# A transformer block in fp32: the first token tiles are split into high and low parts straight from PSUM, and the plain products are issued part by part

## What is computed

```python
def ffn(x, w_gate, w_up, w_down):          # 512 -> 2048 -> 512
    gate = einsum('bsd,hd->bsh', x, w_gate)
    up = einsum('bsd,hd->bsh', x, w_up)
    return einsum('bsh,dh->bsd', silu(gate) * up, w_down)

x = x + 0.5 * ffn(layernorm(x), w_gate, w_up, w_down)
x = x + attn(layernorm(x), W, lam_logit, eta, gamma, beta)   # z = x W', scan, layernorm
x = x + 0.5 * ffn(layernorm(x), w_gate, w_up, w_down)
```

## Time and profile before

| | |
|---|---|
| median of 3 runs | 1061.6 us |
| the profiled execution | 1061.71 us |
| its span in the trace | 1059.9 us |
| TensorE matmul busy | 1048.4 us, 99% |
| VectorE busy | 644.2 us, 61% |
| ScalarE busy | 352.3 us, 33% |
| GpSimd busy | 113.2 us, 11% |
| share of the chain that ended last on TensorE | 96% |

### The profile page before, as it was taken

The page is one execution under the profiler, slowest core; times in us unless marked ns, Lnnn a source line. Parts: engine busy times, 40 slices in busy tenths (PEclk is TensorE's granted clock), DMA queues, the critical chain, the costliest instruction groups (busy, mean ns, idle before and its releaser), DMA issues.

```text
span 1059.9 us, 12841 instructions
## 1 busy us (share of the span) xinstructions
PE 1048.4 (99%) x4756; PEld 867.6 (82%) x4756; DVE 644.2 (61%) x969; ACT 352.3 (33%) x585; POOL 113.2 (11%) x127
## 2 busy tenths in 40 slices
PE   8999999999999999999999999999999999999998
PEld 8788888878888888888888888888888888888886
DVE  5955765567677657878657865687665323233342
ACT  6545544425322222222623222222333332222311
POOL 3322343120020110001002001000000000000000
PEclk9999999999999999999999999999999999999999
DMA  6399877666656556556546555565566566556264
GB/s 196 123 339 339 319 256 262 249 228 199 211 194 211 179 179 199 190 179 212 164 134 227 181 193 179 171 206 179 186 212 217 191 195 200 179 187 210 81 222 164
DMA packets 56845, 215.80 MB, mean 204 GB/s; under 512 B 5840, under 2 KB 15056, under 8 KB 48848
## 3 DMA queue, kind: packets, MB, share of 16 engines
q1 hardware_dynamic: 56640, 214.98, 59.8%
q10 hardware_dynamic: 144, 0.00, 0.0%
HBM read 170.92 MB, written 44.04 MB: 203 GB/s over the span
## 4 chain that ended last, share of the span: by engine, by line
PE 96%; DMA 2%; DVE 1%; DVEq 0%; POOL 0%; issue 0%; SPq 0%
PE ps_a L1275 8%; PE ps_a L1277 8%; PE ps_a L1276 8%; PE ps_b L1277 8%; PE ps_b L1276 8%; PE ps_b L1275 8%; PE ps_d L1275 6%; PE ps_d L1277 6%; PE ps_d L1276 6%; PE ps_c L1275 6%; PE ps_c L1277 6%; PE ps_c L1276 6%; PE aux L1277 3%; PE aux L1275 3%; PE aux L1276 3%; DMA dn<-dn_kept 1%
## 5 line engine op out<-in xcount | busy, mean ns | idle before, releaser
L829 DVE TENSOR_TENSOR tmp<-tmp,ps_c 128x512 f32<-128x512 f32 x59 | 40.5, 687 | 140.4 <-PE ps_c L1277 140.4
L1275 PE MATMUL ps_a<-xt,gu 128*128 128x512 f32 x308 | 121.2, 394 | 2.3 <-DVE gu L873 1.5
L1277 PE MATMUL ps_a<-xt,gu 128*128 128x512 f32 x308 | 120.0, 390 | 0.0
L1276 PE MATMUL ps_a<-xt,gu 128*128 128x512 f32 x308 | 119.9, 389 | 0.0
L1275 PE MATMUL ps_b<-xt,gu 128*128 128x512 f32 x288 | 112.6, 391 | 0.0
L1277 PE MATMUL ps_b<-xt,gu 128*128 128x512 f32 x288 | 112.1, 389 | 0.0
L1276 PE MATMUL ps_b<-xt,gu 128*128 128x512 f32 x288 | 112.1, 389 | 0.0
L1275 PE MATMUL ps_d<-dn,hid 128*128 128x512 f32 x256 | 100.8, 394 | 0.0
L1277 PE MATMUL ps_d<-dn,hid 128*128 128x512 f32 x256 | 99.8, 390 | 0.0
L1276 PE MATMUL ps_d<-dn,hid 128*128 128x512 f32 x256 | 99.7, 389 | 0.0
L1275 PE MATMUL ps_c<-xt,gu 128*128 128x512 f32 x238 | 92.9, 390 | 0.0
(11 more groups left out here) (227 smaller groups left out, 2044.8 us busy)
## 6 DMA issues: line engine op xcount, KB each, us to landing
dn<-dn_kept SPq DMA_DIRECT2D x112, 512.0 KB, 3.3
gu<-gu_kept SPq DMA_DIRECT2D x46, 1024.0 KB, 5.0
gu<-gu_kept SPq DMA_DIRECT2D x46, 768.0 KB, 5.4
gu_kept<-gu SPq DMA_DIRECT2D x16, 1024.0 KB, 4.6
gu_kept<-gu SPq DMA_DIRECT2D x16, 768.0 KB, 4.2
dn_kept<-dn SPq DMA_DIRECT2D x16, 512.0 KB, 5.1
zw<-zw_kept SPq DMA_DIRECT2D x16, 512.0 KB, 3.2
h_t<-w_ffn_in SPq DMA_DIRECT2D x18, 256.0 KB, 4.8
```

The lines of the kernel that those rows point to most:

```text
L829: dve.tensor_tensor(dst, u3s(si), p5_bank(si)[:, :], ALU.add).then_inc(c22_done, 1)
L1275: pe.matmul(dst, a_hi, b_hi, start=start, stop=False, skip_group_check=chained)
L1276: pe.matmul(dst, a_hi, b_lo, start=False, stop=False, skip_group_check=chained)
L1277: return pe.matmul(dst, a_lo, b_hi, start=False, stop=stop, skip_group_check=chained)
```

## The change

Four things are changed, all in the first set pair of pass 0; every later pass has the same instructions in the same order.

1. The high and low parts of the first x operands are made from the PSUM bank of each unit, unit by unit (`hi_first` on ScalarE, `lo_first` on VectorE, eight of 512 columns each), and no longer from `tmp` after four units. B12 gets the place of T4 in `xt`, so `hi_x(0, T4)` now waits for all plain products. `place_x` still copies each bank to `tmp`, for the sums T1 to T4, but behind `lo_first`.
2. `plain` is replaced by `plain_begin` and `plain_end`: four matmuls of weights high by x high, four of weights low by x high, four of weights high by x low, each four with a wait of their own.
3. Units 4 to 7 are turned later (units 4 and 5 behind the third plain product, 6 and 7 inside the fourth), into other banks. The 12 identity matmuls behind unit 3 become 5.
4. The queues of ScalarE and VectorE are reordered to match, and GpSimd's sums of set 4 wait for T4's low part.

```diff
-    KEEP = {1: 2, 3: 12}
+    KEEP = {1: 2, 3: 5}
...
-        first_turn_ps = [ps_d[0], ps_d[1], ps_d[2], ps_d[3], ps_c, ps_d[2], ps_d[3], aux]
+        first_turn_ps = [ps_d[0], ps_d[1], ps_d[2], ps_d[3], ps_a, ps_b, ps_d[2], ps_d[3]]
...
+        def first_part(r, part):
+
+            op = 5 * (r // 4)
+            return xt[:, op:op + 2, part, :, r % 4 * P:(r % 4 + 1) * P]
...
-                ps = {"11": ps_a, "21": ps_b, "12": ps_c, "22": ps_d[2]}[name]
+                ps = {"11": ps_a, "21": ps_b, "12": ps_c, "22": aux}[name]
...
             def place_x(k, r):
                 act.wait_ge(turned_x, 8 * k + r + 1)
+                if k == 0:
+
+                    act.wait_ge(first_lo, r + 1)
                 l, s = r // 4, r % 4
                 act.copy(tmp[:, 4 * l:4 * l + 4, s * P:(s + 1) * P], by_tile(turn_bank(k, r))
                          ).then_inc(placed_x, 1)
 
+            def hi_first(r):
+
+                act.wait_ge(turned_x, r + 1)
+                act.copy(first_part(r, 0), turn_bank(0, r)[:, :].rearrange("p (o k n) -> p o k n", o=2, k=2)
+                         ).then_inc(first_hi, 1)
...
-                if op == B22 and k == 0:
-                    act.wait_ge(placed_x, 8)
+                if op == T4 and k == 0:
+
+                    act.wait_ge(plain_done, 8)
                 act.copy(xt[:, op, 0, :, :], x_raw[op]).then_inc(xhi_ready, 1)
...
+            raw_hi_even(0)
+            for r in range(4):
+                hi_first(r)
+            raw_hi_odd(0)
             place_x(0, 0)
             place_x(0, 1)
-            raw_hi_even(0)
+            raw_hi_even(1)
             place_x(0, 2)
             place_x(0, 3)
-            hi_x(0, B11)
-            hi_x(0, B21)
-            raw_hi_odd(0)
-            raw_hi_even(1)
+            raw_hi_odd(1)
+            first_silu("11")
             norm_first(4)
             norm_first(5)
-            raw_hi_odd(1)
-            first_silu("11")
-            place_x(0, 4)
-            place_x(0, 5)
+            first_silu("21")
+            dn_hi_of(0)
             norm_first(6)
             norm_first(7)
-            first_silu("21")
-            place_x(0, 6)
-            place_x(0, 7)
-            act.wait_ge(placed_x, 8)
-            act.copy(b12_part(0), b12).then_inc(b12_hi, 1)
-            hi_x(0, B22)
+            for r in range(4, 8):
+                hi_first(r)
+            for r in range(4, 8):
+                place_x(0, r)
             hi0(1, 0)
             first_silu("12")
             hi_x(0, T2)
             first_silu("22")
+            gu_hi_a(2)
             hi_x(0, T3)
-            gu_hi_a(2)
+            hi_x(0, T1)
             hi0(1, 1)
-            hi_x(0, T1)
-            dn_hi_of(0)
+            gu_hi_b(2)
             hi_x(0, T4)
-            gu_hi_b(2)
             dn_hi_of(1)
...
+                if k == 4:
+
+                    pool.wait_ge(xlo_ready, parts(0, T4))
                 sums(k)
...
-                ps = {"11": ps_d[0], "21": ps_d[1], "12": ps_d[3], "22": aux}[name]
+                    dve.wait_ge(xlo_ready, parts(0, T2))
+                ps = {"11": ps_d[0], "21": ps_d[1], "12": ps_d[2], "22": ps_d[3]}[name]
...
+            def lo_first(r):
+                dve.wait_ge(first_hi, r + 1)
+                dve.tensor_tensor(first_part(r, 1), turn_bank(0, r)[:, :].rearrange("p (o k n) -> p o k n", o=2, k=2),
+                                  first_part(r, 0).bitcast(F32), ALU.subtract).then_inc(first_lo, 1)
...
+            raw_lo_even(0)
+            for r in range(4):
+                lo_first(r)
+            raw_lo_odd(0)
             stats_x(0, 2)
-            raw_lo_even(0)
+            raw_lo_even(1)
+            raw_lo_odd(1)
             shift_first(2)
-            lo_x(0, B11)
-            lo_x(0, B21)
-            raw_lo_odd(0)
             stats_x(0, 3)
-            raw_lo_even(1)
             shift_first(3)
-            raw_lo_odd(1)
             first_gated("11")
-            dve.wait_ge(b12_hi, 1)
-            dve.tensor_tensor(b12_part(1), b12, b12_part(0).bitcast(F32), ALU.subtract).then_inc(b12_lo, 1)
-            lo_x(0, B22)
+            dn_lo_of(0)
+            for r in range(4, 8):
+                lo_first(r)
             first_gated("21")
             t_of(0, T1)
             t_of(0, T2)
             lo0(1, 0)
             t_of(0, T3)
+            t_of(0, T4)
+            gu_lo_a(2)
             lo_x(0, T2)
-            t_of(0, T4)
             lo_x(0, T3)
-            gu_lo_a(2)
             lo0(1, 1)
+            first_gated("12")
             lo_x(0, T1)
-            first_gated("12")
-            dn_lo_of(0)
+            gu_lo_b(2)
             lo_x(0, T4)
             first_gated("22")
-            gu_lo_b(2)
             dn_lo_of(1)
...
-                    pe.wait_ge(silu11, 1)
+                    pe.wait_ge(placed_x, 5)
...
-                    pe.wait_ge(silu21, 1)
+                    pe.wait_ge(placed_x, 6)
...
-                        pe.wait_ge(silu22, 1)
...
+            def plain_part(dst, u, row, col, w_part, x_part):
...
+                    w = a21_part(u, w_part) if row == 1 and j == 0 else gu[:, u, (A11, A12, None, A22)[2 * row + j],
+                                                                           w_part, :]
+                    x = xt[:, 5 * col + j, x_part, :, :]
                     for k in range(2):
-                        a = slice(k * P, (k + 1) * P)
-                        last = three(dst[:, :], w[0][:, a], w[1][:, a], x[0][:, k, :], x[1][:, k, :],
-                                     j == 0 and k == 0, j == 1 and k == 1)
-                last.then_inc(plain_done, 1)
+                        last = pe.matmul(dst[:, :], w[:, k * P:(k + 1) * P], x[:, k, :],
+                                         start=w_part == x_part == 0 and j == k == 0,
+                                         stop=x_part == 1 and j == k == 1)
+                return last
+
+            def plain_begin(dst, u, row, col):
+                n = 3 * u + (3 if row else 1)
+                pe.wait_ge(first_hi, 4 * col + 4)
+                pe.wait_ge(raw_hi, n)
+                plain_part(dst, u, row, col, 0, 0)
+                pe.wait_ge(raw_lo, n)
+                plain_part(dst, u, row, col, 1, 0)
+
+            def plain_end(dst, u, row, col):
+                pe.wait_ge(first_lo, 4 * col + 4)
+                plain_part(dst, u, row, col, 0, 1).then_inc(plain_done, 1)
...
-                if k == 0 and r in (5, 6):
-                    pe.wait_ge(placed_x, r - 2)
+
+                if k == 0 and r == 4:
+                    pe.wait_ge(silu11, 1)
+                if k == 0 and r == 5:
+                    pe.wait_ge(silu21, 1)
+                if k == 0 and r >= 6:
+                    pe.wait_ge(placed_x, r - 3)
...
-            pe.wait_ge(raw_lo, 1)
-            plain(ps_a, 0, 0, 0)
+            plain_begin(ps_a, 0, 0, 0)
+            plain_end(ps_a, 0, 0, 0)
+            plain_begin(ps_b, 0, 1, 0)
+            plain_end(ps_b, 0, 1, 0)
+            pe.wait_ge(placed_x, 1)
+            plain_begin(ps_d[0], 1, 0, 0)
+            plain_end(ps_d[0], 1, 0, 0)
             turn_x(0, 4)
             turn_x(0, 5)
-            pe.wait_ge(raw_lo, 3)
-            plain(ps_b, 0, 1, 0)
+            pe.wait_ge(placed_x, 2)
+            plain_begin(ps_d[1], 1, 1, 0)
             turn_x(0, 6)
             turn_x(0, 7)
-            pe.wait_ge(raw_lo, 4)
-            pe.wait_ge(placed_x, 1)
-            plain(ps_d[0], 1, 0, 0)
-            pe.wait_ge(raw_lo, 6)
-            pe.wait_ge(placed_x, 2)
-            plain(ps_d[1], 1, 1, 0)
-            pe.wait_ge(placed_x, 5)
-            plain(ps_c, 0, 0, 1)
-            pe.wait_ge(placed_x, 6)
-            plain(ps_d[2], 0, 1, 1)
+            plain_end(ps_d[1], 1, 1, 0)
+            plain_begin(ps_c, 0, 0, 1)
+            plain_end(ps_c, 0, 0, 1)
+            plain_begin(aux, 0, 1, 1)
+            plain_end(aux, 0, 1, 1)
             pe.wait_ge(placed_x, 7)
-            plain(ps_d[3], 1, 0, 1)
+            plain_begin(ps_d[2], 1, 0, 1)
+            plain_end(ps_d[2], 1, 0, 1)
             pe.wait_ge(placed_x, 8)
-            plain(aux, 1, 1, 1)
+            plain_begin(ps_d[3], 1, 1, 1)
+            plain_end(ps_d[3], 1, 1, 1)
```

More of the change, by code:

```diff
@@ L169, in macaron_kernel, with parts @@
         b12 = raw(1, 0)
-        def nth(k, op):
-            order = (B11, B21, B22, T2, T3, T1, T4) if k == 0 else (B11, B21, T2, T3, T1, T4, B22)
-            return order.index(op)
-        def b12_part(part):
-            return zx[:, part, 0:2, :]
+        def parts(k, op):
+            if k == 0:
+                return (T2, T3, T1, T4).index(op) + 1
+            return 4 + 7 * (k - 1) + op + 1
+        def first_part(r, part):
+            op = 5 * (r // 4)
+            return xt[:, op:op + 2, part, :, r % 4 * P:(r % 4 + 1) * P]
         def a21_part(u, part):
@@ L261, in macaron_kernel @@
         raw_lo = sem("raw_lo")
-        b12_lo = sem("b12_lo")
```

(23 more changed lines are left out.)

21 lines of the change are left out of this document (2 added, 19 removed).

## The result

| kernel | median | range | executions |
|---|---|---|---|
| before | 1061.7 us | 1059.97 to 1062.01 | 6 |
| changed | 1055.97 us | 1054.42 to 1057.65 | 6 |

The ratio is 0.9948, with a 95% interval of 0.9937 to 0.9958: 5.7 us off, where 3.9 to 4.0 were forecast. The direction was right, and the time lies in the range, near its lower end. The profiled execution took 1055.73 us, 5.98 less than the one of before.

What follows compares the result with a forecast made beforehand. TensorE, busy 1048.4 of 1059.9 us, was taken as the bound, with gains in its idle time at the start: 2.42 + 1.66 - 0.1 - 0.1 = 3.9 us off, forecast 1057.7, range 1055.6 to 1059.8.

Steps and rivals of the forecast that it cites:

- The first product, 2.42 us earlier: At the start, the first plain product begins at 12.75 in place of 15.17, as the identity matmuls end last.
- The plain stage, 24.02 us: From the first product to the stage's end, 96 matmuls and 16 transposes again take 24.02 us, ending at 36.77.
- The 0.1 charged for the casts of units 6 and 7: In the plain stage, these casts end about 25.5, just when the fifth product needs them; margin about zero, 0.1 us charged.
- The wait of 1.66 us at set 2, gone: Before set 2, `gu_lo_a(2)` is done at 34.2, needed at 36.77, so TensorE's wait of 1.66 us disappears.
- (a): In set 2, `copy_p1(2)` behind `hi_x(0, T4)` ends at 39.2, wanted by `prod6(2)` at 39.5; margin 0.3 us.
- (b): In set 2, ScalarE's copy behind `c11(2)` ends at 44.4, wanted by `prod4(2)` at 44.96; margin 0.5, possible stretches of 0.54.
- the 0.2 charged: The two deductions of 0.1 us each in the sum 2.42 + 1.66 - 0.1 - 0.1.
- Waits for `dn` about as long as before: Later in the kernel, TensorE's waits for `dn` transfers, 3.4 us in the profile before, stay about as long.
- everything behind set 2 waits on TensorE's own progress and shifts as a whole: From set 2 to the end, loads wait for ended products, so all of it moves earlier with set 2.
- the fall near 221: After the 2.26 us wait at 221, the clock runs at 1.2 GHz about 3.4 us, losing 1.7; taken as repeated.
- The rival "not repeated": The clock fall at 221 does not come again, 1.7 us less, 1056.0 in all; 18%.
- The other rivals: New waits, 1058.7 to 1060.2 (12%); gain given back later, 1061.6 (5%); slower, clock falls in plain stage, 1067 (3%).

## Why the prediction was right, and where it was not

**The first product, 2.42 us earlier.** Right: 12.71 against 12.75 worked out, so 2.46. The identity matmuls ended last, as said. Two runs split it: waiting for the low parts costs 1.5, twelve identity matmuls cost 1.6, and five of them in the old kernel bring nothing. So fewer identity matmuls pay nothing by themselves, the new splits and parts with twelve of them bring 0.82 us (14.35 for 15.17), and both together 2.46.

**The plain stage, 24.02 us.** A little less: 36.49 - 12.71 = 23.78. The 24.02 held a wait that I had not seen, for the low part of B22 inside the fifth product, and it makes up the difference. Before:

```profile
29.17 0.40 PE L1277 MATMUL ps_c<-zx,gu 128*128 128x512 f32 x1
29.52 0.50 PE L1275 MATMUL ps_c<-xt,gu 128*128 128x512 f32 x1
29.86 0.40 PE L1276 MATMUL ps_c<-xt,gu 128*128 128x512 f32 x1
```

The starts lie 0.35 and 0.34 apart in place of 0.23, 0.24 us lost. The 0.1 charged for the casts of units 6 and 7 was not lost: they ended at 25.42, 0.09 ahead of `ps_c`. The margin "about zero" was right (`ps_c`'s first weight load had waited for them). Units 4 and 5 could not be turned sooner: before the third product they stall TensorE.

**The wait of 1.66 us at set 2, gone.** Right, and `gu_lo_a(2)` ended at 34.04 (34.2 forecast). The cause was put wrongly in one part: I gave credit to its place in the queue, ahead of two low parts of T's. With the old order the wait is gone as well, by 0.3 us. That the order alone would have removed it is not ruled out.

**Behind set 2.** (a) ended at 38.80 (39.2 forecast) and did not make TensorE wait. (b) ended at 44.72 (44.4 forecast), and `prod4(2)` did wait for it:

```profile
44.15 0.57 ACT L504 COPY tmp<-ps_a 128x512 f32<-128x512 f32 x1
...
44.42 0.39 PE L1296 MATMUL ps_c<-xt,gu 128*128 128x512 f32 x1
...
44.86 0.47 PE L1294 MATMUL ps_a<-xt,gu 128*128 128x512 f32 x1
...
45.17 0.40 PE L1295 MATMUL ps_a<-xt,gu 128*128 128x512 f32 x1
```

The starts lie 0.44 and 0.31 apart in place of 0.23, 0.29 us lost, where before lost 0.18 at the same place: the 0.1 charged was lost there. It is not seen in the shift, since before also lost 0.11 behind set 2's first matmul, which had waited, and the changed kernel did not. The margin of 0.5 was wrong by as much: the sums of set 4 started at 40.73, as forecast, and beside them a small VectorE work ahead of `c11(2)` (line 1279, 128x4) took 0.70 in place of 0.16, the stretch of 0.54 that I had named, while TensorE came for the copy 0.3 sooner. A 1024-column subtraction behind it was stretched to 1.72. In the run with the old order the same place lost 0.17. Up to set 2 the terms add up to 4.36 where 3.9 were forecast: 0.04 from the first product, 0.24 from the stage, and the 0.2 charged, of which nothing was lost by then.

**"Waits for `dn` about as long as before": this step failed.** It held for the wait near 220 (2.51 against 2.26) and not for the late one, 1.16 us, which vanished and is most of what the sum lacked: 4.36 + 1.3 + 0.26 = 5.9. My sentence that everything behind set 2 waits on TensorE's own progress and shifts as a whole left out what does not: transfers like the code packets, whose place against the loads differs from trace to trace. That they are what did away with the late wait here is read from the traces and not tested, and whether its loss belongs to the change or to the build is open: five identity matmuls in the kernel before did away with it as well. So that the whole came out at 5.7 is in part luck; what the change itself was shown to bring is the 4.4. The row of a second wait for `dn` was in the earlier trace rows ("3.4, 2, 2.3"), and I did not ask what ended it.

**The clock.** I took the fall near 221 as repeated in every execution, from four like times. Wrong for both kernels: each has executions with it and without it, 1.7 us apart (4 of 11 without, for the changed kernel). The clearest pair is the changed kernel above, with a wait of 2.51 us and a clock of 0.50 behind it, and the one with the old order, whose profiled execution has the same wait, 2.52 us, and this:

```profile
218.97 0.50 PE L1294 MATMUL ps_a<-dn,zx 128*128 128x512 f32 x1 [2.52 <-DMA dn<-dn_kept]
```

```profile
219.00:220.00 1.00, 1.00 (x4) 1.00 0.97 373
220.00:221.00 1.00, 1.00 (x6) 1.00 1.01 401
```

So after the same wait it fell in one execution and not in the other. By the rule of the Trainium skill (TensorE: Matmul & The Clock Gate, Part 1) that the moment of a change is not tied to the kernel's start and differs from run to run, this is what one would see; the trace agrees. The rival "not repeated" thus described a part of the executions, of either kernel, and nothing of the difference between them; that the measured median lies at its 1056.0 is chance, for both of the middle executions had a fall.

**The other rivals** did not come. Over 12.71 to 36.49 the granted clock is 1.00, new waits cost 0.1 us and not 1, and in pass 0 TensorE waited for no weights.

## What to carry to other kernels

Waiting by parts and filling the gap less go together: a filler matmul costs nothing as long as an operand is late, and all of its time once it is not, so change both and test each alone. Times worked out queue by queue were right to about 0.3 us here, which used up a margin of 0.5, and what went most wrong was a wait a thousand microseconds away that I had listed and not explained: ask of each wait for a transfer what delayed that transfer, before calling it constant. And where a time moves by 1 to 2 us after an edit that can't reach that far, compare executions of one clock level with each other, and look how close to need the loads land, and for a code packet beside them.

## What the runs showed of the hardware

- The program's code arrives while it runs, in 38 or 39 packets of 16 KB, most of them 0.9 to 1.0 us long; the profile books their time as a share of the same 16 DMA engines as the data's. With one 0.76 to 2.04 us ahead of the moment at which TensorE needed a 512 KB load near 220 us, its wait was 2.24 to 2.79 us, and without 1.21 and 1.37. Of the other loads of `dn` that had a packet 1 to 3 us ahead of their usual landing, 22 of 36 took over 0.5 us longer than usual, and of those with no packet near 12 of 1166.
- In kernels whose traced wait near 220 us was 2.2 to 2.8 us, TensorE's clock fell in some executions and not in others (7 of 11 for the changed kernel), to 1.2 GHz for 3.41 us in each trace that has a fall, 1.7 us lost. In the two whose traced wait was 1.21 and 1.37 us it fell in none of 16. Behind a wait of 2.33 us at 15 us (five identity matmuls in the kernel before) the traced execution kept 1.00.
- VectorE's work beside GpSimd's additions: 1.72 us for a 1024-column subtraction in place of 1.21 to 1.23, and 0.70 for one of 128x4 in place of 0.16.
- The last pass's 1 MB store took 7.8 us to land in the kernel before and 6.3 in the changed one and in the kernel before with five identity matmuls. The load of `dn` behind it took 5.1 to 5.2 us in seven traces and 6.1 to 6.5 in the five with a late wait, and 3.2 and 3.7 with the store moved behind it. Why the late wait stood in two kernels whose packet came at another moment stays open.
